# The gates' affine step moves from GpSimd to ScalarE, in a five-engine kernel whose calls are all placed anew

## The reference, cut to what matters

```python
# block 0, mixer: a delta rule over 16 heads of 8, 256 steps in order
a = sigmoid(h @ Wa.T + ba);  b = sigmoid(h @ Wb.T + bb)
S_new = a * S - a * b * outer(S k, k) + b * outer(v, k);  o = q S_new
# block 0, feed-forward: 8 experts of 512 hidden units, top 2 of a router
y = h + sum_e w_e * (silu(h @ we1_e) @ we2_e)
# block 1, mixer: chunked state-space layer ("ssd"); feed-forward ("ffn"): 512 units, gelu
```

## Time and profile before

| | |
|---|---|
| median of 3 runs | 581.25 us (579.19 to 584.04) |
| profiled execution | 579.29 us, span 577.5 us |
| TensorE busy | 449.7 us, 78% |
| VectorE (DVE) busy | 388.0 us, 67% |
| ScalarE (ACT) busy | 379.9 us, 66% |
| GpSimd (POOL) busy | 180.6 us, 31% |
| granted TensorE clock, mean | 0.911 |

### The profile page before, as it was taken

One profiled execution on the slowest core, in us unless ns is written; L12 is line 12 of the kernel. 1 busy time (PEld: TensorE's weight loads), 2 busy tenths in 40 slices (PEclk: granted clock), 3 DMA queues, 4 the chain that ended last, 5 costly groups with the idle time before them and its releaser, 6 DMA issues.

```text
span 577.5 us, 6498 instructions
## 1 busy us (share of the span) xinstructions
PE 449.7 (78%) x2064; PEld 305.5 (53%) x2064; DVE 388.0 (67%) x722; ACT 379.9 (66%) x645; POOL 180.6 (31%) x192
## 2 busy tenths in 40 slices
PE   4666586598765986999888999999799989864045
PEld 3455573376545754676555556677456666441012
DVE  1317897899899997799999579999522292121800
ACT  3688776956976476669737876735986866825242
POOL 0070581793068651046961005123003000030001
PEclk9999788999986999799989999999999999985557
DMA  8956403322410212400320023000000000000000
GB/s 278 359 183 172 129 1 91 92 75 74 123 41 31 61 42 75 121 1 1 91 74 0 2 93 90 0 2 1 0 0 19 1 1 2 0 18 0 0 0 19
DMA packets 34321, 34.13 MB, mean 59 GB/s; under 512 B 12776, under 2 KB 29680, under 8 KB 34032
## 3 DMA queue, kind: packets, MB, share of 16 engines
q1 hardware_dynamic: 34000, 29.52, 17.7%
q10 hardware_dynamic: 288, 4.19, 1.7%
HBM read 30.56 MB, written 3.15 MB: 58 GB/s over the span
## 4 chain that ended last, share of the span: by engine, by line
DVE 42%; PE 21%; ACT 14%; issue 9%; SPq 7%; DMA 4%; POOL 2%; POOLq 0%; DVEq 0%
PE psF L754 6%; DVE R L1803 5%; DVE D L1807 5%; PE psS L772 5%; DVE pbuf L1800 5%; DVE H L1814 4%; DVE D L1801 3%; DVE XX L1786 3%; DVE norm L1783 3%; DVE acc L1827 3%; SPq L527 3%; SPq L478 3%; PE psM L815 2%; ACT L1093 2%; DVE U L1805 2%
## 5 line engine op out<-in xcount | busy, mean ns | idle before, releaser
L772 PEld LDWEIGHTS psS<-we2s,hid 128*128 128x128 f32 x1024 | 136.6, 197 | 59.8 <-issue 48.7
L754 PE MATMUL psF<-h,we1s 128*128 128x512 f32 (+1 forms) x320 | 140.0, 531 | 18.2 <-ACT hid L1280 13.3
L772 PE MATMUL psS<-we2s,hid 128*128 128x128 f32 x1024 | 140.0, 282 | 7.3 <-DVE acc L1827 3.9
L1280 ACT ACTIVATE hid<-psF,col 128x512 f32<-128x512 f32 (+1 forms) x160 | 93.2, 599 | 69.2 <-PE psF L754 68.7
L754 PEld LDWEIGHTS psF<-h,we1s 128*128 128x128 f32 x320 | 56.3, 200 | 46.3 <-issue 23.4
L2194 POOL TENSOR_TENSOR QS<-H,qn 128x512 f32<-128x512 f32 x32 | 45.8, 1440 | 69.0 <-DVE H L1814 49.1
L1827 DVE SCALAR_TENSOR_TENSOR acc<-psS,gate,acc 128x128 f32<-128x128 f32 x128 | 36.2, 339 | 31.7 <-PE psS L772 31.7
L1814 DVE TENSOR_TENSOR_SCAN H<-A,D 128x576 f32<-128x576 f32 x32 | 51.2, 1601 | 1.1
L1095 ACT ACT_TABLE_LOAD x38 | 48.8, 1283 | 1.2 <-issue 0.5
L1800 DVE TENSOR_TENSOR pbuf<-wrep,H 128x512 f32<-128x512 f32 x32 | 30.6, 957 | 12.4 <-issue 5.7
L1093 ACT ACT_TABLE_LOAD x30 | 38.5, 1283 | 0.5
(11 more groups left out here) (191 smaller groups left out, 789.9 us busy)
## 6 DMA issues: line engine op xcount, KB each, us to landing
krep<-scratch_dram SPq DMA_DIRECT2D x64, 128.0 KB, 3.0
wrep<-scratch_dram SPq DMA_DIRECT2D x64, 128.0 KB, 3.0
hid<-fold_mats_dram SPq DMA_DIRECT2D x22, 256.0 KB, 4.0
we1s<-we_dram ACTq DMA_DIRECT2D x1, 2048.0 KB, 9.5
we2s<-we_dram ACTq DMA_DIRECT2D x1, 2048.0 KB, 14.5
outT_dram<-x SPq DMA_DIRECT2D x4, 256.0 KB, 2.6
wrep<-wmod_dram SPq DMA_DIRECT2D x1, 768.0 KB, 5.5
scratch_dram<-kn SPq DMA_DIRECT2D x3, 256.0 KB, 2.0
```

The source lines that it names most:

```text
L754: mm(bank[name][:, 0:ncols(w)], we1s[:, e, k * P:(k + 1) * P], h2[w % 2][:, 0:ncols(w)], start=True, stop=True).then_inc(s_hid_mm, 1)
L772: last = mm(bank[name][:, t * P:(t + 1) * P], hid[n % 2][:, k, t * P:(t + 1) * P], we2s[:, e, k, :], start=(k == 0), stop=(k == HT - 1))
L1280: nc.scalar.activation(hid[x_ % 2][:, k, 0:c], psF[n % 2][:, 0:c], ACT.Silu, bias=pc("be1", HT * e + k)).then_inc(s_hid_done, 1)
```

## The change

The POOL function `gates` is gone. A new ACT function `halve` does the affine step right behind each Tanh, by an Identity activation with scale 0.5 and a bias of 0.5 that is read from a third column of `eps`. The order of the calls on all engines is new. Core of the diff:

```diff
-        eps = sb("eps", P, 2)
+        eps = sb("eps", P, 3)
...
+            def halve(g, i):
+
+                act.wait_ge(s_gate_raw, i)
+                nc.scalar.activation(g, g, ACT.Identity, bias=eps[:, 2:3], scale=0.5).then_inc(s_gates_done, 1)
...
                         nc.scalar.activation(ag[n % 2][:, 0:ncols(n)], ps[:, 0:ncols(n)], ACT.Tanh, bias=hab[:, 0:1],
                                              scale=0.5).then_inc(s_gate_raw, 1)
+                        halve(ag[n % 2][:, 0:ncols(n)], 2 * n + 1)
...
                         nc.scalar.activation(bg[:, 0:ncols(n)], ps[:, 0:ncols(n)], ACT.Tanh, bias=hab[:, 1:2],
                                              scale=0.5).then_inc(s_gate_raw, 1)
+                        halve(bg[:, 0:ncols(n)], 2 * n + 2)
...
+                v_.memset(eps[:, 2:3], 0.5).then_inc(s_eps_set, 1)
...
-            def gates(n):
-
-                k = ncols(n)
-                pool.wait_ge(s_gate_raw, 2 * (n + 1))
-                for t in (ag[n % 2], bg):
-                    g_.tensor_scalar(t[:, 0:k], t[:, 0:k], 0.5, 0.5, ALU.mult, ALU.add).then_inc(s_gates_done, 1)
```

Of the new order, the pieces that the prediction speaks of. On SP, `spread_keys(1)` stands before `spread_solved(1)`. On TensorE (`-` before, `+` now), around the start of window 2's experts and around the first view of block 1:

```diff
             router(2)
             logits(2)
-            for s in range(27, 30):
+            for s in range(27, 31):
                 slot(1, s)
-            project(4, 4)
-            slot(1, 30)
             gate_rows(2)
             slot(1, 31)
...
             attn_out(4)
-            for s in range(14, 21):
+            slot(2, 15)
+            slot(2, 16)
+            ssd_in(0)
+            for s in range(17, 24):
                 slot(2, s)
-            ssd_in(0)
...
             ssd_out(0)
             router(3)
-            slot(2, 28)
+            key_products(4, 3)
             center(("ffn", 0))
             variance(("ffn", 0))
-            slot(2, 29)
-            slot(2, 30)
+            for s in range(28, 31):
+                slot(2, s)
```

On DVE, in window 3 and in block 1's first view:

```diff
             chunk(3, 0)
             mix_expert(1, 6)
-            convolve(4)
             mix_expert(1, 7)
             chunk(3, 1)
+            convolve(4)
             experts_branch(1)
...
             chunk(3, 7)
+            mix_expert(2, 3)
             ssd_decay(0)
-            mix_expert(2, 3)
             ssd_mix(0)
             couple(4, 0)
+            ln(("moe", 3))
+            mix_expert(2, 4)
+            ssd_norm(0)
             couple(4, 1)
-            ln(("moe", 3))
-            ssd_norm(0)
             couple(4, 2)
-            ssd_halo(1)
             ssd_branch(0)
-            mix_expert(2, 4)
             couple(4, 3)
```

## The result

The changed kernel takes **586.83 us** (median of 20 runs, 583.33 to 590.29), the kernel before 580.51 us (20 runs, 578.49 to 585.77): ratio **1.0102, 95% interval 1.0083 to 1.0121**, so about 6 us slower, where no change was forecast. The profiled execution took 585.05 us with a span of 583.3 us.

A forecast was written before the change was run, and what follows sets the result against it. No single engine bounds the whole: VectorE sets 60.3 to 244 us, TensorE 244 to 509. Terms 0.2 + 1.5 + 0 - 2.0 = -0.3 us, from 579.29 to 579.0 us; range 569.5 to 587.

The forecast's parts named there:

- The gates: Ten POOL operations become ACT Identities; shorter VectorE state copies: minus 1.0 us, bounds minus 3.7 to plus 6.3.
- Window 1: Keys' spread sent earlier, chunk(1,0) ahead of route(0), hiding router latency: minus 1.3 us, bounds minus 2.8 and plus 1.3.
- Window 3's first chunks: convolve(4) moved behind chunk(3,1), so VectorE newly waits 2.5 us for expert 7: plus 1.4, bounds 0 and plus 4.1.
- Block 1's first view: Earlier gains end at the wait for mix_expert(2,2); level at 325 us plus 0.2, bounds minus 3 and plus 3.
- The Gelus: Two more table loads in each of the first two views: plus 1.5 us in the first, 0 in the second.
- Window 3's waits: Three waits, center of ("ssd", 1), ssd_in(1) and mix_expert(3,4), have their cause moved away: minus 2.0 us.
- The slower rival: ACT's added Identities and table loads make TensorE wait for psF evacuations: 587 us, chance 0.15.

The follow-up runs named there:

- e1: Kernel before, order of calls kept, only the gates' ten halvings moved from POOL to Identities on ACT: 580.19 us, ratio 0.9984 to the kernel before.
- r4: Changed kernel with route(0) back ahead of chunk(1,0) on VectorE, nothing else moved: 588.95 us, ratio 1.0135 to the kernel before.
- g2: Changed kernel's order up to about 258 us, the kernel before's order behind, halvings on ACT: 584.18 us, ratio 1.0050 to the kernel before.
- e3: Changed kernel with the gelus of views 0 and 1 together again on ACT, TensorE's slots around them as before: 590.66 us, ratio 1.0168.
- g1: Kernel before's order up to about 258 us, the changed kernel's order behind, halvings on ACT: 586.95 us, ratio 1.0098 to the kernel before.
- s2: Kernel before's order except from 258 to 296 us, which has the changed kernel's order; halvings on ACT: 582.91 us, ratio 1.0049.
- t1: As s2, but on ACT attn_branch(5) ahead of ssd_exp(0), nothing else moved: 579.50 us, ratio 0.9980 to the kernel before.
- g4: Changed kernel with only view 0's gelus together again on ACT, view 1 still split: 584.48 us, ratio 1.0055 to the kernel before.
- r3: Old order to 350 us, changed kernel's to router(4), old to ffn_down(1), changed kernel's behind; halvings on ACT: 581.94 us, ratio 1.0022.
- r1: Changed kernel with the old order from 296 to 350 us, view 0's gelus together: 586.12 us, ratio 1.0089 to the kernel before.
- e2: Changed kernel's order of all calls, but the halvings kept on POOL, none on ACT: 592.10 us, ratio 1.0211 to the kernel before.
- s4: Old order to 258 us, changed kernel's behind, view 0's gelus together again, halvings on ACT: 584.71 us, ratio 1.0047 to the kernel before.

## Why the prediction was wrong

The gates. Forecast minus 1.0; e1 measured minus 0.9 us (interval minus 2.3 to plus 0.5). Right in size, though zero lies inside the interval. The reason given shows in e1's profile, where the 32 state copies took 20.6 us together instead of 22.6; in the changed kernel they took 22.5, so the new order gave that back. The Identities took 722 and 508 ns, 6.4 us together, where the neighbour row gave 6.3 as the most.

Window 1. `chunk(1,0)` started at 102.03 us as forecast (100 to 102). But `solve(2)` came 0.4 us later, not 1.3 earlier. VectorE only exchanged two pieces of its own work: `route(0)` began 6.8 us later and took 6.3 us instead of 5.3, with POOL beside it. r4 shows that exchanging them back is no gain either. Single profiles scatter too much here to say more: up to chunk(3,0) the new front shows neither the forecast gain nor a loss, and in run times it is left open (g2).

Window 3's first chunks. The new wait behind `chunk(3,0)` was 1.37 us where 2.5 was forecast; one of 0.49 us ahead of `convolve(4)` came with it. Forecast plus 1.4; from `chunk(3,0)` to `chunk(3,2)`, behind both, it is 17.66 us where it was 16.71: plus 0.9 (the same 16.7 in e1, the same 17.7 in e3). Right.

**Block 1's first view: the step that failed.** "Level at 325 us: plus 0.2", with bounds of minus 3 and plus 3; it was plus 4.8 at logits(3). The 0.2 was VectorE's lead of 0.9 and a loss of 1.05 in the view; in these two profiles VectorE was 2.2 late at `chunk(3,2)`, and the view lost 2.6 from there. The lead never came, but its absence is not the loss: g1, with the old order up to 258 us, loses all of it. The prediction took the wait for `mix_expert(2,2)` as the point where TensorE and VectorE meet, and counted `ssd_in(0)` done ahead of it as harmless or a gain. The meeting point that mattered was the next one, the centre of moe 3, which hangs on ACT's queue: `attn_branch(5)` behind `ssd_exp(0)` behind `ssd_decay(0)`. The prediction saw what was put into VectorE's list there and never asked who stands behind ssd_exp(0) on ACT. s2 prices the stretch at 3.8 us and t1 shows the wait to be its cause there.

The full new order has the same chain. `attn_out(5)` ends at 304.67 us, and its Identity runs at 307.41:

```profile
306.77 0.63 ACT L1298 ACTIVATE ssdb<-ssdb 128x512 f32<-128x512 f32 x1 [1.97 <-DVE ssdb L1922]
307.31 0.20 ACT L1300 ACTIVATE f<-t 128x16 f32<-128x16 f32 x1
307.41 0.46 ACT L1241 ACTIVATE br<-psB,col 128x256 f32<-128x256 f32 x1
```

But `key_products(4,0)` and `slot(2,25)` now lie between as well, and the wait is 2.18 us and not 6.05. What it costs there was not run, and the profiles give no single price. The changed kernel, e3 and g4 have the same code up to router(3) and the same waits (4.0 us for `acc`, 2.1 to 2.2 for POOL), and take 65.8, 64.1 and 67.0 us from `chunk(3,2)` to router(3); the granted clock over the last 26 to 29 us of it is 0.91, 0.97 and 0.84. So against the old order's 64.1 to 64.6 the stretch costs from nothing to 3 us there, more where the clock is lower. Of the changed kernel's 6 us, the split gelus are shown (2.7, g4); the division of the rest stays open.

The Gelus. Forecast plus 1.5 for the first view and 0 for the second. The profile gives 19.92 us from logits(3) to the end of ffn_down(0), against 18.38: plus 1.54, with the wait of 1.33 us inside `ffn_down` at the place and nearly the size named (1.4). In the run times the split costs 2.0 to 3.0 us, within the bounds of 0 and 3.5. Second view: plus 0.16 us once the extra slot is taken off. Right.

Window 3's waits. Forecast minus 2.0; the level fell from 6.4 to 4.8. Right.

So each of these terms came close to its forecast. The sum was minus 0.3 and the profile says plus 5.8; 4.6 of the 6.1 us between them were there at logits(3), the rest is made of small amounts behind it, such as 0.6 us from the end of ffn_down(1) to the end of the kernel. The slower rival's mechanism, TensorE waiting for `psF` evacuations, did not occur: waits on `hid` there fell from 5.6 to 2.5 us.

```profile
PE psS L772 <- DVE acc L1830: 4.0, 1, 4.0
PE psA L593 <- POOL x L2203: 3.0, 2, 2.2
PE psF L754 <- ACT hid L1279: 2.5, 5, 1.5
```

Its time (587 us) was nearly right by luck: ACT did hold up TensorE, but through the order of its queue and not through its load. There are 76 table loads of 1283 ns as forecast, and again no drain of 1380 ns shows beside them, which the Trainium skill, ScalarE: Activation LUTs, section "What ACT_TABLE_LOAD costs", adds to every switch; in the sequence below the gelu ends at 341.65 by the 0.69 us of its row, and the load starts at 341.67:

```profile
339.67 1.28 ACT L1087 ACT_TABLE_LOAD   x1
340.96 0.69 ACT L1316 ACTIVATE ssdb<-psM,ubias 128x512 f32<-128x512 f32 x1
341.67 1.28 ACT L1087 ACT_TABLE_LOAD   x1
342.96 0.69 ACT L1279 ACTIVATE hid<-psF,col 128x512 f32<-128x512 f32 x1
343.67 1.28 ACT L1085 ACT_TABLE_LOAD   x1
```

## What to carry to other kernels

When calls are placed anew, follow every queue from the moved call: who stands right behind it on its own engine, on each engine that it feeds, and how many calls the bounding engine has left to fill the time. A small operation of another chain behind one that waits (an Identity of 0.45 us behind exps) cost 3.8 us in s2, and swapping the two was the whole cure. Work moved ahead of a wait is not a gain if it was the cover of the wait after it. And price an order change by whole stretches, run one by one: single gains of 1 to 2 us from different profiles did not survive gluing (r3, r1).

## What was not expected of the hardware

- An Identity on ACT from SBUF to SBUF, 128x512 f32 in place with a bias from a column and a constant scale, took 722 ns, and 508 ns for 256 columns; Exp in place on 512 columns took 630 ns.
- A VectorE TENSOR_TENSOR of 64 columns took 0.21 us alone and 1.30 us beside a POOL operation; POOL's run of products, begun 0.6 us earlier against the routing step, went with a step of 9.4 us instead of 6.3 (e2).
- Behind a wait of 6.05 us the same two centre matmuls took 2.08 us, behind 0.64 us 1.13 us; the granted clock from 300 to 320 us was 0.83 in s2, and 1.00 in e1 and t1. A wait can cost TensorE more than its length, but need not: behind 2.07 us in g4 these matmuls took 1.97 us, behind 2.14 us in e3, the same code up to there, 1.13 us.
- Profiles of kernels with the same code up to there differed by 1.5 us at `solve(0)` (44.59 us in the changed kernel, 46.10 in e3), where four matmuls at 23 us (L630 and L632) took 1.25 and 1.91 us, and by 5.7 us at chunk(3,0) (237.81 us in g1, 243.52 in s4). Times read off single profiles compare no better than that in this front; behind it most stretches repeat to 0.2 us between kernels with the same order.
